# The second layer's attention output kept in 32 bits for its output projection, instead of split in two 16-bit halves

## What is computed

```python
scores = jnp.einsum('bnqhd,bnkhd->bnhqk', q, k) / np.sqrt(HD)
probs = jax.nn.softmax(scores, axis=-1)
attn = jnp.einsum('bnhqk,bnkhd->bnqhd', probs, v).reshape(B, nW, W, D)
attn = jnp.einsum('bnwd,ed->bnwe', attn, out_w) + out_b
x = _layernorm(x + attn, ln1_g, ln1_b)
```

## Time and profile before

| | |
|---|---|
| median of 3 runs | 2314.04 us (2309.74 to 2316.64) |
| the profiled execution | 2316.24 us, of which 2314.5 us from the first to the last instruction |
| TensorE busy | 2141.3 us, 93% |
| ScalarE busy | 1736.7 us, 75% |
| VectorE busy | 1698.6 us, 73% |
| GpSimd busy | 1272.5 us, 55% |
| granted TensorE clock, mean | 0.986 of full |

### The profile page before, as it was taken

How to read it: one execution, slowest core, us unless ns; L and a number is a source line. 1 busy time by engine, 2 the same in 40 slices (tenths; PEclk the granted TensorE clock), 3 DMA queues, 4 the chain that set the end, 5 groups by cost and what they waited for, 6 DMA issues and landing times. The chain is left out here.

```text
span 2314.5 us, 59631 instructions
## 1 busy us (share of the span) xinstructions
PE 2141.3 (93%) x21394; PEld 1563.5 (68%) x21394; DVE 1698.6 (73%) x5284; ACT 1736.7 (75%) x3393; POOL 1272.5 (55%) x1576
## 2 busy tenths in 40 slices
PE   4899999999999999999999999999999999999984
PEld 2667666677766677766677766677766667766663
DVE  6677777777787777777777777777787777787753
ACT  2678777878777878777877777878777878777863
POOL 5256555566555566555556555556555556555554
PEclk8999999999999999999999999999999999999997
DMA  1111111111111111111111111111111111111110
GB/s 45 23 43 32 38 44 46 29 42 29 39 43 46 30 42 29 39 43 46 31 42 29 39 42 46 31 42 32 37 42 46 33 40 33 36 41 46 35 31 19
DMA packets 76188, 86.84 MB, mean 38 GB/s; under 512 B 20624, under 2 KB 55440, under 8 KB 76048
## 3 DMA queue, kind: packets, MB, share of 16 engines
q1 hardware_dynamic: 62368, 52.44, 9.4%
q10 hardware_dynamic: 13680, 33.04, 4.3%
HBM read 18.29 MB, written 16.78 MB: 15 GB/s over the span
## 5 line engine op out<-in xcount | busy, mean ns | idle before, releaser
L993 PEld LDWEIGHTS ps<-vg,p 128*128 128x128 f32 x4096 | 511.5, 192 | 51.9 <-issue 12.9
L993 PE MATMUL ps<-vg,p 128*128 128x129 f32 x4096 | 537.9, 278 | 0.7 <-ACT p L544 0.7
L392 POOL TENSOR_SCALAR nmean<-mv 128x4 f32<-128x4 f32 x256 | 58.3, 228 | 575.3 <-DVE mv L763 572.0
L544 ACT ACTIVATE p<-ps 128x512 f32<-128x512 f32 x512 | 300.2, 587 | 91.1 <-PE ps L887 90.6
L725 DVE TENSOR_REDUCE cm<-ps 128x1 f32<-128x512 f32 x512 | 334.0, 679 | 15.5 <-PE ps L949 13.9
L537 ACT ACTIVATE ps<-shift 128x512 f32<-128x512 f32 x512 | 300.9, 596 | 17.4 <-ACT p L544 0.7
L428 POOL TENSOR_TENSOR e<-e,srec 128x512 f32<-128x512 f32 x128 | 134.0, 1047 | 241.5 <-DVE srec L808 241.5
L394 POOL TENSOR_TENSOR rstd<-veps,halfpow 128x4 f32<-128x4 f32 x256 | 265.8, 1038 | 0.0
L1089 PE MATMUL ps<-w,hid 128*128 128x128 f32 x2048 | 242.2, 277 | 5.2 <-ACT hid L596 2.0
L1089 PEld LDWEIGHTS ps<-w,hid 128*128 128x128 f32 x2048 | 233.5, 192 | 8.6 <-ACT hid L596 8.6
L587 ACT ACTIVATE oh<-ps 128x512 f16<-128x512 f32 x64 | 38.2, 597 | 240.2 <-PE ps L1057 240.2
(11 more groups left out here) (180 smaller groups left out, 5501.3 us busy)
## 6 DMA issues: line engine op xcount, KB each, us to landing
ptbd<-et SPq DMA_DIRECT2D x512, 64.0 KB, 2.0
kbd<-kk SPq DMA_DIRECT2D x512, 32.0 KB, 2.0
out_y<-o_sb ACTq DMA_DIRECT2D x64, 256.0 KB, 2.0
x_sb<-in_x ACTq DMA_DIRECT2D x31, 512.0 KB, 4.0
x_sb<-in_x SPq DMA_DIRECT2D x1, 512.0 KB, 3.5
e<-in_w_t SPq DMA_DIRECT2D x1, 256.0 KB, 3.6
w<-in_w_t SPq DMA_DIRECT2D x1, 256.0 KB, 3.6
hid<-in_in_w_t SPq DMA_DIRECT2D x1, 192.0 KB, 2.5
```

Source lines behind the costliest of these rows:

```text
L544: sc.activation(p32[:, c % PRING, :], bank("st", c), ACT.Exp, scale=C ** -0.5).then_inc(s["p_made"], 1)
L993: last = mm(ps[:, b, at:at + PVW], p32[:, c % PRING, part], vg32[:, j, :], start=j == 0 and q % 2 == 0, stop=j == MT - 1, skip_group_check ...
```

## The change

ScalarE writes the attention output as 32 bits into a new tile `o32`. VectorE's subtraction is gone. The output weights are kept in 32 bits in `wo`, by one copy at the start instead of two halves. `out` on TensorE waits for ScalarE's `o_hi` and issues one matmul of 32-bit operands for each 128 tokens: 4 instead of 12. The next user of the bank of `pv0` waits for `o_hi` instead of `o_lo`. The orders are otherwise the same.

```diff
     "dve": """
-        k:1-- max:4- max:5- max:6- max:7- maxima:0- pv1:0-- max:8- q:1-- out:0-- max:9- max:10- score0:1--
-        score1:1-- prob0:1-- turn_mid:0-- max:11- turn_p0:1-- prob1:1-- turn_p1:1-- max:12- down:0-- pv1:1-- out:1--
+        k:1-- max:4- max:5- max:6- max:7- maxima:0- max:8- q:1-- out:0-- max:9- max:10- score0:1--
+        score1:1-- prob0:1-- turn_mid:0-- max:11- turn_p0:1-- prob1:1-- turn_p1:1-- max:12- down:0-- out:1--
...
-    "score0": ("sub_made", 2, True), "score1": ("sub_made", 2, True), "pv0": ("o_lo", 1, True),
+    "score0": ("sub_made", 2, True), "score1": ("sub_made", 2, True), "pv0": ("o_hi", 1, True),
...
+        wo = sb("wo", [P, P])
...
-        oh, ol = sb("oh", [P, 2, HALF], F16), sb("ol", [P, 2, HALF], F16)
+        o32 = sb("o32", [P, 2, HALF])
...
                 act.wait_ge(s["pv_win_mm"], upto(2 * img + h))
-                sc.activation(oh[:, h, :], bank("pv0", h), ACT.Copy).then_inc(s["o_hi"], 1)
+                sc.activation(o32[:, h, :], bank("pv0", h), ACT.Copy).then_inc(s["o_hi"], 1)
...
-                halves(OUT)
+                link(v_.tensor_copy(wo[:], wraw[:, OUT, :]))
...
-            def pv1(kind, img, h):
-                dve.wait_ge(s["o_hi"], upto(2 * img + h))
-                v_.tensor_tensor(ol[:, h, :], bank("pv0", h), oh[:, h, :], ALU.subtract).then_inc(s["o_lo"], 1)
...
             def out_proj(kind, img, h):
                 claim(kind, img, "out", h)
-                pe.wait_ge(s["o_lo"], upto(2 * img + h))
+                pe.wait_ge(s["o_hi"], upto(2 * img + h))
                 for j in range(HT):
                     part = slice(P * j, P * (j + 1))
-                    last = three(bank("out", h)[:, part], oh[:, h, part], ol[:, h, part], wh[:, OUT, :], wl[:, OUT, :])
+                    last = mm(bank("out", h)[:, part], o32[:, h, part], wo[:], start=True, stop=True)
                 last.then_inc(s["out_mm"], 1)
```

More of the change, by code:

```diff
@@ L253, in build @@
             q_hi q_lo k_hi k_lo v_made score_mm smax_made sub_made exp_made ssum_made srec_made prob_made
-            et_made pv_win_mm o_hi o_lo out_mm y_bias y1_made r1_scaled r1_made m_hi m_lo
+            et_made pv_win_mm o_hi out_mm y_bias y1_made r1_scaled r1_made m_hi m_lo
             up_mm hid_made down_mm y2_made t2a_made t2b_made t2_made scaled clipped
@@ L861, in _ @@
                       "turn_in": turned_lo("turn_in", "x_hi", "x_lo"), "q": q, "k": k, "score0": score(0),
-                      "score1": score(1), "prob0": prob(0), "prob1": prob(1), "turn_p0": turn_p(0), "turn_p1": turn_p(1), "pv1": pv1, "out": out_proj,
+                      "score1": score(1), "prob0": prob(0), "prob1": prob(1), "turn_p0": turn_p(0), "turn_p1": turn_p(1), "out": out_proj,
                       "turn_mid": turned_lo("turn_mid", "m_hi", "m_lo"), "down": down, "ln_q": ln_q,
@@ L1123 @@
 SETUP_PSUM = SETUP_FIRST + 1 + 4 + 2
-SETUP_STEPS = SETUP_PSUM + 4 + 1 + 1 + 2 + 2 + 2 + 1 + 1 + 1 + 1 + 1 + 1 + 1 + 1 + 2
+SETUP_STEPS = SETUP_PSUM + 3 + 1 + 1 + 2 + 2 + 2 + 1 + 1 + 1 + 1 + 1 + 1 + 1 + 1 + 2
 def kernel(**inputs):
```

## The result

The change makes the kernel slower. Median of the kernel with the change 2320.6 us, of the kernel before 2313.7 us in the runs beside it; ratio 1.0033 with a 95% interval of 1.0025 to 1.0042, so 7.6 us more (5.8 to 9.7). The forecast was 2304.4 us, 9.6 less. The measured time is about that of the rival to which the prediction gave 3 in 100, four passes for each 32-bit product: 2320 there, worked out as 5.9 us more.

The account below looks back on a forecast made before the run. TensorE's own list, busy 93% of the span, was taken as the bound. 31 images x 0.27, the last image 0.9 and the start 0.3 gave 9.6 us off 2314.04, so 2304.4 us; 8-in-10 range 2296 to 2313.

Parts of the forecast that it names:

- four passes: Rival: each 32-bit product in out costs four 56 ns passes, 0.90 us per out, total 2320 us; chance 0.03.
- the cost of the matmuls: TensorE's out: four 32-bit matmuls at 112 ns, priced from down, take 0.45 us, 0.22 less per half.
- Half 1 keeps everything: At out:1, y and turn_mid:1 come 0.27 us earlier per image, all of it kept; bounds 0.22 to 0.33.
- Half 0 keeps nothing: After out:0, TensorE is 0.38 us ahead but st:0 still waits for ScalarE's seed; kept 0.
- VectorE's subtractions are worth their waits only: Removing VectorE's 64 subtractions, 43.9 us of its time, is priced at 0 beyond the waits counted elsewhere.
- ScalarE's write of 32 bits costs nothing: ScalarE's attention-output copy stays at 0.60 us, as the negation writing 32 bits of the same shape takes 0.60.
- The last image: On the chain through out:1 that ends last, y starts at 2271.96 instead of 2272.89, 0.93 us earlier.
- The start: In weight preparation, one copy replaces a copy and a subtraction, saving between 0.1 and 0.7 us, taken as 0.3.
- The collision of transfers: Rival: before pv1:1, the next image's load delays the probabilities' DMA, giving 2344 us; chance 0.05.

Follow-up runs that it names:

- half 1 alone: Two 16-bit products instead of three in out:1 only, without VectorE's step for it, against the kernel before: 0.996, 9.2 us less.
- with two products there: Two 16-bit products instead of three in out:0 only, without VectorE's step for it, against the kernel before: 1.0006 (0.9995 to 1.0017).
- the kernels that prepare both forms: 32-bit out without VectorE's step in one half only, the other in 16 bits, against the kernel before: out:0 only 1.0008, out:1 only 1.0018.
- with two products: Two 16-bit products instead of three in out of both halves, without VectorE's subtraction, against the kernel before: 0.9966, 7.9 us less.

## Why the prediction was wrong

**The step that failed is the cost of the matmuls**, its first and largest term: 4 x 112 = 0.45 us for the new `out`, where it is 8 x 111 = 0.89. The rows were right and were divided by the wrong number. The 32 matmuls of `down` in the earlier trace rows were taken for 32 products, each "exactly the new form". `down` has 4 x 4 = 16 products per half; with 64 halves that is 1024, and the group of the earlier trace rows stands there with x2048. Had the count of the row been held against the loops of the code, two instructions per product would have been plain before any run. The other 32-bit products say the same: `pv` has 2048 in the code and x4096 in its group, `pv_win` likewise. The transposes show the opposite case: `turn_in` and `turn_mid` (L1005) together have 4 x 64 x 2 = 512 in the code and 512 in their group of the profile, one instruction each, though their operands have 32 bits too.

The Trainium skill, "FP8 and Floating Point Precision", section "TensorE Precision Notes", has four passes for a true 32-bit product. The prediction set that aside because 112 ns is two distances of 56 ns. A product takes 2 x 112 = 224 ns, which is four of 56, and the rule holds for the time in this trace.

What follows from the wrong term, point by point:

- *Half 1 keeps everything.* Right as a mechanism: with `out` at 0.45, half 1 alone gave 9.2 us (6.5 to 11.8), where 31 x 0.27 + 0.9 = 9.3 was worked out. With `out` at 0.89 the same mechanism hands on the loss, 0.17 per image.
- *Half 0 keeps nothing.* Right for a gain: with two products there the time did not fall, and the idle time before `st:0`'s load grew by 0.30. The earlier start of `out:0` was set at 0.16 and is 0.14. The row that decided it was the 0.24 us of idle time ended by ScalarE's seed beside the 0.02 of slack. The same reading says that a loss isn't swallowed, and 0.06 of it was not.
- *VectorE's subtractions are worth their waits only.* Right: 2.5 us (0.2 to 4.9) against 2.3 expected.
- *ScalarE's write of 32 bits costs nothing.* Right: 0.60 us in both traces (597 ns in the group of each).
- *The last image.* The wait for VectorE was there, the size was off with the matmuls: 0.44 less instead of 0.93.
- *The start.* Set at 0.3, and there: TensorE waits 8.15 us for the end of VectorE's chain of preparations instead of 8.47 (8.74 in the kernels that prepare both forms). It can't be told from the times. TensorE, idle for over 8 us before, then runs on average at 0.58 (before) and 0.51 (after) of the full clock for the next 5.3 and 5.9 us, near the lower level of 1.2 GHz, and how long that lasts varies by more than 0.3 us from trace to trace.
- *The collision of transfers.* Not seen: the matmuls waited 14.6 us for the probabilities before and 11.4 after, and the longest wait was 1.5 instead of 1.8.

The rival of four passes was worked out at 0.17 us per image for half 1 and 0.06 for half 0, which is what the trace shows, and at 7.1 us for the images and 5.9 in all; the measured 7.6 (5.8 to 9.7) has that size. Its chance of 0.03 was the second mistake: one number, the distance of two instructions, carried all the weight against it, and nothing else in the profile had been asked.

## What to carry to other kernels

Before a duration from a profile is taken as the price of an operation, divide the row's count by the number of times that the code issues the operation; here one 32-bit product was two matmul instructions of 112 ns, and three products of split 16-bit parts (168 ns) were cheaper than it (224 ns). A saving on a full engine counts only up to the next wait that another engine sets: in this kernel 0.38 us were worth nothing in half 0 and 0.27 their full size in half 1, and the idle time ended by ScalarE's seed told so beforehand.

## What was not expected of the hardware

A row of eight 32-bit matmuls takes 0.89 us (111 ns each) behind other 32-bit matmuls, and 0.97 us when it stands behind a wait: the distance from the first start to the second is then 0.18 us, about the 0.19 of one weight load. A wait isn't needed for it: `pv:3` takes 0.95 directly behind a row of 16-bit matmuls of 128 columns (before, and with two products), its first distance being 0.17. That in both cases the first load has too little time to run ahead is the likely reading; no run varied the load. The twelve 16-bit matmuls, with loads of 97 ns, take 0.67 us with the wait and without it. So a wait before 32-bit matmuls was dearer here than the same wait before 16-bit ones, by 0.07 us each time.
